# One graph-attention layer on one core: the order of the first stage's work is rewritten on four engines

## What is computed

```
h      = relu(layernorm(x))                       # sources, [2048, 256]
hs, ht = layer_norm(h), layer_norm(h_target)      # with scale and bias, masked by node
q      = (ht @ Wq + bq) / sqrt(32)
k, v   = hs @ Wk + bk, hs @ Wv + bv
logits = where(adj != 0, q k^T, -1e30)            # per head, [2048, 2048]
ctx    = softmax(logits) v
ht     = layer_norm(ht + ctx @ Wo + bo)           # masked
out    = x + ht + gelu(ht @ W1) @ W2
```

## Time and profile before

| what | value |
|---|---|
| median of three runs | 692.8 us (689.97, 692.81, 692.8) |
| the profiled execution's own time | 694.41 us |
| its span in the trace | 692.6 us |
| PE busy | 657.6 us, 95% of the span |
| DVE, POOL, ACT busy | 569.2, 524.2, 484.0 us |
| granted TensorE clock, mean | 0.993 |

### The profile page before, as it was taken

The page is one execution under the profiler, slowest core; times in us unless marked ns, Lnnn a source line. Parts: engine busy times, 40 slices in busy tenths (PEclk is TensorE's granted clock), DMA queues, the critical chain, the costliest instruction groups (busy, mean ns, idle before and its releaser), DMA issues. The chain is left out here.

```text
span 692.6 us, 20346 instructions
## 1 busy us (share of the span) xinstructions
PE 657.6 (95%) x8346; PEld 473.0 (68%) x8346; DVE 569.2 (82%) x946; ACT 484.0 (70%) x932; POOL 524.2 (76%) x488
## 2 busy tenths in 40 slices
PE   4898999999999999999999999999999899899998
PEld 4465667766776777677767766777777567557767
DVE  5987899989999879999997798989868888575661
ACT  4865668766778858677787686778866788867550
POOL 3574889889999957899998678999977777471430
PEclk9998999999999999999999999999999999999999
DMA  8735501113001011220011112012000000000001
GB/s 296 258 80 153 177 31 36 59 63 108 2 2 34 2 62 63 58 82 2 2 33 33 62 33 78 17 51 74 2 2 2 2 3 2 1 1 32 24 17 54
DMA packets 20797, 36.23 MB, mean 52 GB/s; under 512 B 2752, under 2 KB 13280, under 8 KB 20704
## 3 DMA queue, kind: packets, MB, share of 16 engines
q1 hardware_dynamic: 20704, 34.92, 16.2%
HBM read 26.49 MB, written 2.10 MB: 41 GB/s over the span
## 5 line engine op out<-in xcount | busy, mean ns | idle before, releaser
L1412 POOL TENSOR_TENSOR prob_lo<-prob 128x512 f16<-128x512 f32 x382 | 437.1, 1169 | 74.1 <-ACT prob L888 73.2
L888 ACT ACTIVATE prob<-score 128x512 f32<-128x512 f32 x512 | 304.1, 597 | 135.8 <-PE score L469 128.3
L469 PE MATMUL score<-nidentb,mask_nat 128*128 128x128 bf16 x2048 | 199.1, 220 | 4.1 <-ACT qT L905 1.9
L469 PE MATMUL early<-kT,qT 96*128 96x512 f16 x512 | 192.9, 382 | 10.5 <-DVE half_max L1203 10.1
L469 PEld LDWEIGHTS ctx<-v_sb,prob 128*128 128x128 bf16 x2048 | 159.0, 98 | 60.2 <-ACT raw L910 12.6
L469 PE MATMUL score<-qT,kT 97*128 97x512 f16 x512 | 196.3, 383 | 0.0
L1203 DVE CUSTOM_DVE_ANT_0 early<-early,mask_nat,half_max 128x1024 f32<-128x1024 f32 x128 | 163.6, 1287 | 38.0 <-PE early L469 36.0
L469 PE MATMUL ctx<-v_sb,prob 128*128 128x65 f16 x2048 | 191.4, 193 | 2.3 <-ACT raw L910 1.8
L469 PE MATMUL ctx<-v_sb,prob_lo 128*128 128x65 f16 x2048 | 190.4, 193 | 0.0
L469 PEld LDWEIGHTS ctx<-v_sb,prob_lo 128*128 128x128 f16 x2048 | 142.6, 97 | 49.9 <-issue 4.0
L1203 DVE CUSTOM_DVE_ANT_0 early<-early,mask_nat 128x1024 f32<-128x1024 f32 x128 | 157.1, 1229 | 22.5 <-PE early L469 20.8
(11 more groups left out here) (167 smaller groups left out, 623.2 us busy)
## 6 DMA issues: line engine op xcount, KB each, us to landing
adj_in<-in_adj SPq DMA_DIRECT2D x26, 512.0 KB, 4.0
qT<-q_stage SPq DMA_DIRECT2D x48, 64.0 KB, 2.0
kT<-mask_nat SPq DMA_DIRECT2D x48, 64.0 KB, 2.0
raw<-in_x SPq DMA_DIRECT2D x4, 512.0 KB, 5.6
tgt<-in_L_gnn_h_target SPq DMA_DIRECT2D x4, 512.0 KB, 11.6
prob<-in_adj SPq DMA_DIRECT2D x4, 512.0 KB, 10.4
nT<-in_L_gnn_W SPq DMA_DIRECT2D x2, 1024.0 KB, 6.6
mask_nat<-in_x SPq DMA_DIRECT2D x1, 2048.0 KB, 8.3
```

Source lines behind the costliest of these rows:

```text
L469: return nc.tensor.matmul(dst, w, m, start=start, stop=stop, **more)
L888: nc.scalar.activation(prob[:, n % SLOTS, :], score[n % 2][:, :], ACT.Exp).then_inc(exp_done, 1)
L1412: nc.gpsimd.tensor_tensor(prob_lo[:, n % SLOTS, :], prob[:, n % SLOTS, :], prob_hi(n % SLOTS), ALU.subtract).then_inc(lo_sem["pool"], 1)
```

## The change

It moves calls within the four lists, and adds 24 products on PE.

- PE: `project` takes the halves that it is to do. `turn_rows(3)` and `turn_rows(4)` now stand between the two halves of `project(2)` and `project(3)`. Ahead of `project(2, (0,))` stand 24 products of 128x128 that nobody reads (`UNREAD_LATER`), into `early[1]`. `values(2)` moves from before pair 0 to behind pair 2, pair 1 moves ahead of `project(4)`, and each of pairs 2 to 7 is followed by one `values`. `shift_row(0)` stands before pair 9 instead of behind it.
- ACT: `features` goes ahead of `deviation`, `high_parts` and `last_sources`; `target_deviation(1)`, `(2)` and the table for Exp move behind `high_values(5)`; `high_values(7)` moves behind `row_out(0)`.
- DVE: `low_parts(0)` goes ahead of `second_scale(2)`, the first mask ahead of `low_parts(2)`; `target_stats(1)` and `(2)` move from between the low parts to either side of `maxima(4)`.
- POOL: `drop_sources(1)` goes ahead of `source_norm(2)`.

```diff
--- before.py
+++ after.py
@@ -47,7 +47,7 @@
 PLACE = 3 * 16
 
 
-WIDE, UNREAD = 64, 20
+WIDE, UNREAD, UNREAD_LATER = 64, 20, 24
 
 
 GROUPS = ("t0", 0, 1, 2, 3)
@@ -483,7 +483,7 @@
                             last = nc.tensor.transpose(score[c][:, t * P:(t + 1) * P], tile, ident32[:, :])
                         last.then_inc(tp_ready, 1)
 
-                def project(g):
+                def project(g, halves=range(DC)):
                     what = GROUPS[g]
                     if what == "t0":
                         pe.wait_ge(wq_scaled, 1)
@@ -493,7 +493,7 @@
                         pe.wait_ge(nT_masked, DC * (what + 1))
                     if g == 1:
                         pe.wait_ge(bc_done, 1)
-                    for m in range(DC):
+                    for m in halves:
                         if g == 0 and m == 1:
 
                             pe.wait_ge(q_b, 1)
@@ -688,21 +688,26 @@
                 project(1)
                 turn_rows(2)
                 values(0)
+                for i in range(UNREAD_LATER):
+                    mm(early[1][:, TB:TB + P], identb[:, :], identb[:, :], True, True)
+                project(2, (0,))
                 turn_rows(3)
-                project(2)
+                project(2, (1,))
                 values(1)
+                project(3, (0,))
                 turn_rows(4)
-                project(3)
-                values(2)
-                for i in range(2):
-                    early_scores(0, i)
-                project(4)
-                for e in range(1, RAMP + 2):
+                project(3, (1,))
+                for e in range(2):
                     for i in range(2):
                         early_scores(e, i)
-                    if e + 2 < NT // 2:
-                        values(e + 2)
-                shift_row(0)
+                project(4)
+                for e in range(2, RAMP + 2):
+                    if e == RAMP + 1:
+                        shift_row(0)
+                    for i in range(2):
+                        early_scores(e, i)
+                    if e < NT // 2:
+                        values(e)
                 for n in range(AHEAD):
                     scores(n)
                     if n in (1, 3):
@@ -997,30 +1002,30 @@
                 deviation(1)
                 high_parts(0)
                 rectify(3)
+                features(2)
                 deviation(2)
                 high_parts(1)
-                features(2)
+                high_values(0)
                 deviation(3)
-                last_sources()
-                high_values(0)
                 features(3)
                 high_parts(2)
+                last_sources()
                 high_values(1)
                 features(4)
                 high_parts(3)
+                high_parts(4)
+                high_values(2)
+                feature_sum(0)
+                feature_sum(1)
+                for i in range(3, 6):
+                    high_values(i)
                 for k in range(1, 3):
                     target_deviation(k)
                 nc.scalar.activation(warm_c, eps_c, ACT.Exp).then_inc(act_link, 1)
-                high_values(2)
-                high_parts(4)
-                feature_sum(0)
-                high_values(3)
-                high_values(4)
-                feature_sum(1)
-                for i in range(5, NT // 2):
-                    high_values(i)
+                high_values(6)
                 negated(0)
                 row_out(0)
+                high_values(7)
                 for n in range(AHEAD):
                     exponential(n)
                 mean_high()
@@ -1281,31 +1286,32 @@
                 second_scale(1)
                 first_stats(3)
                 second_stats(2)
+                low_parts(0)
                 second_scale(2)
                 second_stats(3)
                 second_scale(3)
-                low_parts(0)
                 low_parts(1)
                 low_values(0)
+                make_mask(0, 0)
+                low_parts(2)
+                for i in range(1, TT):
+                    make_mask(0, i)
+                low_values(1)
+                low_parts(3)
+                maxima(0)
+                maxima(1)
+                low_parts(4)
+                maxima(2)
+                low_values(2)
+                make_mask(0, 4)
+                maxima(3)
+                make_mask(0, 5)
                 target_stats(1)
-                low_parts(2)
+                maxima(4)
                 target_stats(2)
-                low_values(1)
-                for i in range(2):
-                    make_mask(0, i)
-                low_parts(3)
-                for i in range(2, TT):
-                    make_mask(0, i)
-                maxima(0)
-                low_values(2)
-                low_parts(4)
-                maxima(1)
-                make_mask(0, 4)
-                maxima(2)
-                make_mask(0, 5)
-                for e in range(3, RAMP + 1):
+                for e in range(5, RAMP + 2):
                     maxima(e)
-                for e in range(RAMP + 1, RAMP + FILL):
+                for e in range(RAMP + 2, RAMP + FILL):
                     maxima(e)
                 mean_low()
 
@@ -1469,8 +1475,8 @@
                 pool.wait_ge(bc_done, 2)
                 drop_sources(0)
                 source_norm(1)
+                drop_sources(1)
                 source_norm(2)
-                drop_sources(1)
                 drop_sources(2)
                 drop_sources(3)
                 nc.gpsimd.memset(v_sb[:, :, :, 2 * HD:VS], 1.0).then_inc(zeroed, 1)
```

## The result

The median went from 692.8 to 689.34 us over six runs each (689.1 to 690.26 after, 689.97 to 693.06 before): ratio 0.996, 95% interval 0.9944 to 0.9977. The medians are 3.5 us apart, about half of the 6.3 forecast; the means, to which the ratio belongs, are 2.7 us apart. That is small, and just on the edge of what a measurement of this kernel can tell. The profiled execution went from 694.41 to 689.24, by 5.2 us. These two differences are not the same, and that is the heart of this case.

What follows compares the result with a forecast made beforehand. PE bounds the unchanged main part, so the gain is PE reaching scores(5) sooner: 4.6 us at scores(0) plus 1.7 after it, 6.3 in all, taking the median from 692.8 to 686.5; range 683.5 to 690.8.

Steps and rivals of the forecast that it cites:

- the sum's last line: Gain of 6.3 us takes the profiled 694.4 to 688.1; the same difference from the 692.8 median gives 686.5.
- step 1: PE's second turn: gap half filled, clock doesn't fall, project(2) ends at 33.8 instead of 36.85, 3.0 us gained.
- step 4: Shift and first scores: scores(0) at 60.25, scores(5) at 64.65, 6.26 us ahead, 1.7 of that from this step.
- Step 2: Third turn to end of project(4): it ends at 44.45 instead of 48.48, net gain 2.75 us.
- Step 3: Maxima: DVE's chain, now with two target statistics, holds PE; maxima 7 ends at 58.75 instead of 62.48, gain 3.7 us.
- A: Clock falls again near 57 to 62 us, as DVE's chain runs late: gain 3.8, time 689.0; chance 0.17.
- B: Clock falls behind a turn, as transposes don't count as PE being busy: gain 3.5, time 689.3; chance 0.08.
- D: Work hidden anyway: keys land late or POOL's group 3 masking binds, project(4) starts near 43; 688.5; chance 0.10.
- C: Slower: DVE binds early, PE waits for maxima 4 and 5, clock falls at 53: 695.5; chance 0.05.

Runs made afterwards that it cites:

- the filler: Kernel before with only 24 unread products added ahead of turn_rows(3), no call moved: 690.27 us, ratio 0.9987.
- the kernel with the early statistic: Changed kernel with target_stats(1) moved from ahead of maxima(4) to ahead of low_parts(3): 687.91 us, ratio 0.9931.

## Why the prediction was half right

**The step that failed is the sum's last line:** "the same difference from 692.8 gives 686.5". It took a difference from one execution, at clock 0.993, and subtracted it from a median of executions that mostly had lost less to the clock. Of the 5.2 us that lie between the two profiled executions some 4.4 are the two stretches at 1.2 GHz, since the same change gives 0.7 to 0.8 where neither kernel has them. The trace with the filler gives the same, step by step: of step 1's 2.9 us 1.65 are clock (project(2) ends at 35.20 there), and the way from scores(0) to scores(5), 6.09 us at 1.2 GHz, takes 3.98 in the old order at full clock, so step 4's saving was all clock and the new order is 0.5 us longer there. The falls are real in the execution whose trace I read. But 19 of 47 executions of the kernel before had none of them. The three times shown before, 689.97, 692.81 and 692.8, beside 694.41 for the profiled one, are four values on three of the levels; I read them as scatter of 2.8 us about one time. (By its own terms the range began at 683.7 and not 683.5.)

**Step 1** was right: 3.0 us forecast, 2.9 measured against the same trace (33.91 instead of 36.85). The unread products took 1.34 us (27.76 to 29.10) for 1.3. What they were to bring was wrong: without them the time is the same.

**Step 2** was right to 0.4 us (44.81 for 44.45); pair 0 waits for the keys, as worked out. I missed that pair 4 waits for the keys of groups 2 and 3.

**Step 3** had the right mechanism, DVE's chain, and was 1.0 us short: 59.7 for 58.75, 0.8 of it by the one mask. That is the term of the first stage's sum that was mis-sized: 0.62 us forecast, 1.45 measured. I called the statistics a cost, yet took them as given; the two runs on them show that one alone is worth 1.4 us. That term is why the new order, 2.0 us ahead at project(4), is only 0.7 ahead in the end. The rule that I weighed there, from the Trainium skill ("GPSIMD Engine Reference", Specifications), is half borne out. The late masks came beside or behind POOL's own mask, and took 1.45 and 0.68; before, two took 0.64 each beside it. Neither "always slow" nor "never" holds. POOL's row says more:

```profile
41.96 7.35 POOL L1442 TENSOR_SCALAR mask_nat<-prob_lo 128x1024 bf16<-128x1024 int32 x2
```

POOL's second mask ends at 49.31, and DVE's slow mask at 49.86, 0.55 us behind it, which is nearly the whole of an undisturbed mask. The mask of 1.22 us in the kernel before also ends 0.55 us behind the POOL instruction beside it (54.17 and 53.62), and so does the one of 1.07 in the trace with the filler (52.52 and 51.97). A mask that begins under the end of a POOL instruction looks as if it waits for that end. The two of 0.64 us, in the middle of POOL's first mask, didn't, and why not stays open.

**Step 4.** From scores(0) to scores(5) it took 4.45 us for the 4.4 forecast. ACT's copies stood as expected:

```profile
61.26 0.60 ACT L879 ACTIVATE raw<-score 128x512 f32<-128x512 f32 x1
61.89 0.63 ACT L882 ACTIVATE v_sb<-raw 128x512 f16<-128x512 f32 x1
62.42 1.07 ACT L893 ACTIVATE prob<-score 128x512 f32<-128x512 f32 x2
```

**Rivals.** A and B didn't come: no execution of the changed kernel fell below 1.0. B's rule (the Trainium skill, "TensorE: Matmul & The Clock Gate", Part 4: PE-mode transpose) would have shown behind the turn at 31.27 or 37.44. The mean clock of 1.00 up to scores(5) shows nothing there, so these two turns alone didn't do it. D's price, 0.3 and 0.55 us of waiting for keys, was smaller than 2 us. C came only in the experiments.

## What to carry to other kernels

Before subtracting from a median, ask whether the profiled execution is one of the median's kind: its time, its mean clock and the spread of the other runs say so, and if the times stand in steps, each step is a state and the gain has to be worked out for each. A reordering that keeps TensorE busy can be worth more by the clock states that it removes than by the path it shortens. Work moved off one path lands somewhere: here a statistic taken out of a gap and put into the chain of maxima cost 1.4 of the 2.1 us that the rest of the order gave at full clock, and the same trace showed the idle 1.88 us that it had left.

## What the runs showed of the hardware

One and the same code ran at six levels between 690 and 697.9 us on one chip, by how often TensorE was at 1.2 GHz. The same three waits (1.15, 0.60 and 0.68 us) came with 6.7 us at 1.2 GHz from about the second on in one execution, and with no fall in the execution with the filler. The moves to and from full clock also come at varying times elsewhere. In the execution profiled of the kernel with the early statistic, the first transposes still ran slowly at 14.38, the next at the full rate at 17.36, and it lost clock once more in the steady part:

```profile
14.38 1.91 PE L483 MATMUL score<-ident,tgt 128*128 128x128 f32 x8
...
17.36 1.05 PE L483 MATMUL score<-ident,raw 128*128 128x128 f32 x8
```
```profile
14.00:16.00 2.00, 2.00 (x14) 2.00 (x12) 1.93 (x8) 0.52 (x1) 1.71 (x3) 1.00 1.03 399
...
530.00:540.00 10.00, 8.23 (x102) 5.54 (x99) 7.14 (x13) 7.13 (x12) 5.66 (x6) 0.83 0.01 2
```

Eight transposes took 1.91 us there, and 1.05 from 17.36 on; with this first rise the mean granted clock has nothing to do, as the window from 14 to 16 us shows 1.00 all the same. In the changed kernel's trace the first transposes, at 13.60, already took 1.05 us. That execution took 689.68 us, and the eleven others of its kernel 687.8 to 688.1. Other kernels have executions 1 us above the rest at clock 1.0 (690.26 for the changed one); whether these are late first rises too no trace shows.
